# A graph layer on one core: bias of the late tiles through the early sums, key rows of two groups loaded together, loops written out

## What is computed

```python
xn = _layernorm(x)
# messages over 16 relations, summed at the destination
transformed = einsum('ni,rio->rno', xn, weight)
gnn = segment_sum(transformed[rel_type, src] * norm, dst)
# linear attention over all nodes, with a gate
q, k, v = split(xn @ Wqkv)
k = softmax(k, axis=nodes)
context = einsum('bnhd,bnhv->bhdv', k, v)
out = einsum('bnhd,bhdv->bnhv', q, context)
gate = sigmoid(gelu(xn2 @ Wg1 + bg1) @ Wg2 + bg2)
x = x + gnn + (out * gate @ Wproj + bproj)
# mixture of 8 experts, the two best of each row
x = x + moe(_layernorm(x))
```

## Time and profile before

| | us |
|---|---|
| three runs | 1664.4, 1661.96, 1661.58 |
| median of the runs | 1661.96 |
| the profiled execution, span from first to last instruction | 1663.3 |
| early tiles, per tile (from 85 to 297) | about 12.4 |
| late tiles, 22 of them from 357 to 730.7 | 373.7 |
| 22 pairs of phase two, from 843.7 to 1590.5 | 746.8 |

### The profile page before, as it was taken

One profiled execution on the slowest core, in us unless ns is written; L12 is line 12 of the kernel. 1 busy time (PEld: TensorE's weight loads), 2 busy tenths in 40 slices (PEclk: granted clock), 3 DMA queues, 4 the chain that ended last, 5 costly groups with the idle time before them and its releaser, 6 DMA issues.

```text
span 1663.3 us, 38419 instructions
## 1 busy us (share of the span) xinstructions
PE 1611.3 (97%) x10484; PEld 1452.9 (87%) x10484; DVE 1354.3 (81%) x3387; ACT 968.4 (58%) x2178; POOL 1043.2 (63%) x1134
## 2 busy tenths in 40 slices
PE   6999999999999999998699999999999999999998
PEld 5788888788888788786599999999999999999998
DVE  7978565488888888884579999999999999999985
ACT  4444222346556555553566777676767777676764
POOL 3543231577878787775677767776767766767730
PEclk9999999999999999999899999999999999999999
DMA  8676765688888888887633333333333333333320
GB/s 264 213 258 242 249 251 209 224 269 268 265 266 274 256 257 266 267 264 257 185 98 109 100 113 103 102 104 114 98 97 110 101 110 101 106 101 114 98 60 10
DMA packets 126969, 289.13 MB, mean 174 GB/s; under 512 B 21271, under 2 KB 49724, under 8 KB 126914
## 3 DMA queue, kind: packets, MB, share of 16 engines
q1 hardware_dynamic: 86068, 177.19, 29.3%
q0 software_dynamic: 39952, 110.13, 24.7%
q10 hardware_dynamic: 894, 1.16, 0.2%
HBM read 149.49 MB, written 138.90 MB: 173 GB/s over the span
## 4 chain that ended last, share of the span: by engine, by line
PE 71%; issue 8%; POOL 8%; DMA 4%; DVE 4%; ACT 2%; ACTq 0%; DVEq 0%; POOLq 0%
PE bank L1743 56%; POOL raw L673 6%; PE bank L1941 4%; DMA raw<-table,idxa 3%; PE bank L1942 3%; PE bank L1784 2%; PE bank L1785 1%; ACT mh L995 1%; POOL xres L638 1%; PE bank L1893 1%; DMA slot<-kv_d 1%; PE bank L1991 1%; PE bank L1979 1%; DVE ml L1523 1%; PE bank L1795 1%
## 5 line engine op out<-in xcount | busy, mean ns | idle before, releaser
L787 POOL DMA_INDIRECT stg<-table,idxcur x495 | 538.2, 1087 | 245.2 <-issue 111.5
L1743 PE MATMUL bank<-wreg,xt 128*128 128x512 f32 x2352 | 590.2, 402 | 4.6 <-DVE wreg L1136 1.9
L1743 PEld LDWEIGHTS bank<-wreg,xt 128*128 128x128 f32 x2352 | 436.6, 190 | 99.7 <-DVE stg L1178 2.3
L673 POOL DMA_INDIRECT raw<-table,idxa x297 | 308.6, 1039 | 86.5 <-issue 77.4
L1743 PE MATMUL bank<-tt,wreg 128*128 128x256 f32 (+1 forms) x2400 | 322.6, 284 | 2.4 <-DVE tt L1589 2.2
L1743 PE MATMUL bank<-wreg,ht 128*128 128x256 f32 x2352 | 316.8, 283 | 0.2 <-DVE ht L1639 0.2
L1743 PEld LDWEIGHTS bank<-tt,wreg 128*128 128x128 f32 x2400 | 299.8, 190 | 7.6 <-issue 7.3
L1743 PEld LDWEIGHTS bank<-wreg,ht 128*128 128x128 f32 x2352 | 295.1, 188 | 0.4 <-DVE ht L1639 0.4
L1051 ACT ACTIVATE raw<-bank,cols 128x256 f32<-128x256 f32 (+1 forms) x400 | 164.6, 462 | 105.1 <-PE bank L1743 105.1
L1523 DVE SCALAR_TENSOR_TENSOR ml<-stg,nrm,mh 128x256 fp32r<-128x256 f32 x455 | 196.1, 477 | 21.5 <-ACT mh L995 21.3
L1178 DVE COPY stg<-bank 128x512 f32<-128x512 f32 x196 | 133.4, 685 | 94.5 <-PE bank L1743 93.8
(11 more groups left out here) (236 smaller groups left out, 2151.5 us busy)
## 6 DMA issues: line engine op xcount, KB each, us to landing
table<-stg SPq DMA_DIRECT2D x196, 512.0 KB, 3.5
kv_d<-kvs SPq DMA_DIRECT2D x49, 256.5 KB, 4.5
xt_d<-xt SPq DMA_DIRECT2D x49, 256.0 KB, 4.1
xtp<-xt_d SPq DMA_DIRECT2D x24, 512.0 KB
stg<-table,idxcur POOLq DMA_INDIRECT x495
sk<-kv_d SPq DMA_DIRECT2D x24, 256.5 KB, 5.7
out_x<-xres SPq DMA_DIRECT2D x24, 256.0 KB
xres<-in_x POOLq DMA_DIRECT2D x23, 256.0 KB, 4.3
```

Of the source, the lines that this page charges most:

```text
L673: pool.indirect_dma_start(ring_a[:, r * EARLY + j, :], None, table[0:LIMIT, :], bass.IndirectOffsetOnAxis(ap=idxa[:, at:at + 1], axis=0)). ...
L787: pool.indirect_dma_start(stg[:, (s % 4) * SUP + j, :], None, table, bass.IndirectOffsetOnAxis(ap=idxcur[:, at:at + 1], axis=0)).then_inc( ...
L1743: mm = pe.matmul(dst, stat(a, c), mov(b, c), start=(n == 0), stop=(n == 3 * chunks - 1))
```

## The change

1. *Bias.* POOL's `early_gathers` no longer calls `add_bias`, so tiles 24 to 48 get no bias from POOL. DVE prepares two rows in tile 19 (`bias_rows`: high part in row 0 and low part in row 32 of `bp2`, zeros between). PE adds them by one matmul with a matrix of ones at the head of `early_sums` in odd rows, from tile BIAS_FROM = 36 on, which covers the tiles 24 to 48. `ones` becomes fp32r. DVE's `early_add` waits for POOL's bias only once.
2. *Key rows.* A new tile `later` of 14 slots lies where `wreg` begins; groups 1 and 2 are loaded into it behind group 0 without waiting for contexts. The work is cut into six parts of four or three tiles, two at slot 0 and one each at slots 1 to 4 of pair 0. The context is finished at slot 5, and the steps after it move one slot ahead. `split_hi` of the first chunk waits for all contexts. SP loads pair 0 ahead of the first two chunks. POOL's head mask and the indices of the second half of pair 0 move ahead of its gathers.
3. *Loops.* Every `Fori` of both phases becomes a Python loop, on all five engines.

```diff
+    BIAS_FROM = K2 + K2 // 2
+    BP_LO = 32
         xres = sb("xres", [P, NT, C], F32)
+        with ExitStack() as begun:
+            later = sb("later", [P, 2 * SLOTS, KVW], F32, begun)
         wreg = sb("wreg", [P, 2, 4, CC, WC, C], F32R)
...
-        ones = sb("ones", [P, P], F32)
+        ones = sb("ones", [P, P], F32R)
...
+        def group_of(part):
+            return part // 2
+        def span_of(part):
+            return (4, SLOTS) if part % 2 else (0, 4)
+        def rows_of(part):
+            g = group_of(part)
+            return slot if g == 0 else later[:, SLOTS * (g - 1):SLOTS * g]
...
-            with sp.Fori(K2 // 2 + 1, NP - 1) as i:
+            for i in range(K2 // 2 + 1, NP - 1):
...
-            def load_group(g):
-                for n, k in enumerate(group(g)):
-                    if g:
-                        sp.wait_ge(ctx_mm, HELD + SLOTS * (g - 1) + n + 1)
-                    elif n == 5:
+            def load_rows(part):
+                a, b = span_of(part)
+                for n in range(a, b):
+                    if part == 1 and n == 5:
                         sp.wait_ge(ctx1_mm, KEPT)
-                    sp.dma_start(slot[:, n, :], kv_d[k]).then_inc(kv_in[n], 16)
-            load_group(0)
+                    sp.dma_start(rows_of(part)[:, n, :], kv_d[group(group_of(part))[n]]).then_inc(kv_in[part], 16)
+            load_rows(0)
+            load_rows(1)
             first_phase_over(sp)
-            for g in range(1, GROUPS):
-                load_group(g)
-            load_chunk(4)
-            sp.wait_ge(k1_dve, 6)
-            load_chunk(5)
+            for part in range(2, 2 * GROUPS):
+                load_rows(part)
...
             load_pair(0, 2)
+            load_chunk(4)
+            sp.wait_ge(k1_dve, 6)
+            load_chunk(5)
...
-                    if r == 2:
-                        add_bias(k)
...
             first_phase_over(pool)
+            heads()
+            next_indices(0, 0, 2)
+            next_indices(0, 1, 2)
             for h in range(PIECES):
                 pool.wait_ge(tbl_st[h], 16 * NT)
...
+                if (i, s) == SPLITS[0]:
+                    act.wait_ge(ctx_mm, HELD + REST)
                 if (i, s) in SPLITS:
                     split_hi(4 + SPLITS.index((i, s)))
...
+            def bias_rows():
+                dve.wait_ge(bp_in, 16)
+                dve.memset(halves(bp2[:]), 0.0).then_inc(late_lo, 1)
+                dve.wait_ge(late_lo, 2)
+                for row in (0, BP_LO):
+                    dve.tensor_copy(bp2[row:row + 1, :], bpb[row:row + 1, :]).then_inc(late_lo, 1)
+                dve.wait_ge(late_lo, 4)
+                dve.tensor_tensor(bp2[BP_LO:BP_LO + 1, :], bpb[BP_LO:BP_LO + 1, :], halves(bp2[BP_LO:BP_LO + 1, :]),
+                                  ALU.subtract).then_inc(late_lo, 1)
...
-                dve.wait_ge(bias_in, min(t + 1, NT) if isinstance(k, int) else t + 1)
+                if isinstance(k, int) and k == K2:
+                    dve.wait_ge(bias_in, K2)
...
-            def early_sums(k, i, b, r):
+            def early_sums(k, i, b, r, biased):
...
                 pe.wait_ge(selected_a, q + 1)
+                if biased:
+                    pe.wait_ge(late_lo, 5)
+                    pe.matmul(bank[7][:, 0:C], ones[0:BP_LO + 1, :], bp2[:], start=True, stop=False)
...
-                        early_sums(k, i, b, j // 2)
+                        early_sums(k, i, b, j // 2, bias and j // 2 % 2 == 1)
...
+            for first, last, bias in ((K2 // 2 + 1, BIAS_FROM // 2, False), (BIAS_FROM // 2, NP - 1, True)):
+                for i in range(first, last):
+                    tile_pe(2 * i, i, 0, (2 * i + 1, 1), rows, bias)
+                    tile_pe(2 * i + 1, i, 1, (2 * i + 2, 0), rows, bias)
...
-                if isinstance(i, int) and (i, s) == (0, 6):
+                if isinstance(i, int) and (i, s) == (0, 5):
                     context_turn()
                     context_values()
-                if isinstance(i, int) and (i, s) == (0, 7):
+                if isinstance(i, int) and (i, s) == (0, 6):
                     query_context()
...
-GROUP_SLOTS = (0, 1, 3)
+PARTS_OF_SLOT = {0: (0, 1), 1: (2,), 2: (3,), 3: (4,), 4: (5,)}
...
-    with eng.Fori(2, pairs) as i:
+    for i in range(2, pairs):
         for s in range(8):
             slot_of(i, s, 8, i - 1, 2, i - 2, 2)
```

More of the change, by code:

```diff
@@ L575, in _ @@
             load_pair(1, 2)
-            with sp.Fori(2, NP) as p:
+            for p in range(2, NP):
                 load_pair(p, 2)
@@ L1727, in gate_bias @@
                     pe.matmul(bank[5][:, 0:G], lnbb[:, c, :], wg1_raw[:, c, :], start=(c == 0), stop=False)
-                pe.matmul(bank[5][:, 0:G], ones[0:1, :], bg1r, start=False, stop=True).then_inc(setup_pe, 1)
+                pe.matmul(bank[5][:, 0:G], halves(ones[0:1, :]), bg1r, start=False, stop=True).then_inc(setup_pe, 1)
             def query_turn():
@@ L1817, in tile_pe @@
                     pe.wait_ge(k1_dve, 1 + CC)
-                    pe.matmul(bank[7][:, 0:C], ones[:], dg1, start=True, stop=True).then_inc(k1_pe, 1)
+                    pe.matmul(bank[7][:, 0:C], halves(ones[:]), dg1, start=True, stop=True).then_inc(k1_pe, 1)
                 if isinstance(k, int) and STAGES < k <= STAGES + 3:
@@ L1874, in _ @@
             pe.wait_ge(k_shift_diag, 2)
-            pe.matmul(bank[1][:, 0:C], ones[:], dg[:], start=True, stop=True).then_inc(kmb_mm, 1)
+            pe.matmul(bank[1][:, 0:C], halves(ones[:]), dg[:], start=True, stop=True).then_inc(kmb_mm, 1)
             pe.wait_ge(add_a, ALL_ADDS)
@@ L1879, in _, with held_contexts @@
             contexts_kept(NT - 1, NP, 1, 3)
-            def contexts(g):
-                for b in range(0 if g else HELD):
+            def held_contexts():
+                for b in range(HELD):
                     pe.wait_ge(k_exp, b + 1)
@@ L1888, in contexts @@
                     mm.then_inc(ctx_mm, 1)
-                for part_no, first, last in parts(g):
-                    pe.wait_ge(k_exp, part_no + 1)
-                    for n in range(first, last):
-                        for c in range(CC):
-                            mm = pe.matmul(bank[2 + c][:, 0:XW], slot[:, n, c * P:(c + 1) * P],
-                                           slot[:, n, C:KVW], start=False, stop=(group(g)[n] == NT - HELD - 1))
-                        mm.then_inc(ctx_mm, 1)
+            def contexts(part):
+                rows = rows_of(part)
+                pe.wait_ge(k_exp, HELD + part + 1)
+                for n in range(*span_of(part)):
+                    for c in range(CC):
+                        mm = pe.matmul(bank[2 + c][:, 0:XW], rows[:, n, c * P:(c + 1) * P], rows[:, n, C:KVW],
+                                       start=False, stop=(group(group_of(part))[n] == NT - HELD - 1))
+                    mm.then_inc(ctx_mm, 1)
             def context_turn():
@@ L2037, in slot_of @@
                     if i + s == 0:
-                        contexts(0)
+                        held_contexts()
+                        for part in PARTS_OF_SLOT[0]:
+                            contexts(part)
                     if (i, s) == (1, 6):
@@ L2108, in in_slot, with run @@
                 steps[name](p, nt, *map(int, expert))
[L2111 removed]
+def run(slot_of, pairs, tail_groups):
     for s in range(8):
```

176 lines of the change are left out of this document (81 added, 95 removed).

## The result

The changed kernel takes 1634.67 us (median of 4 runs, 1631.11 to 1636.7) against 1663.18 us for the kernel before in the same set (4 runs, 1661.58 to 1665.61): a ratio of 0.9826 [0.9809, 0.9842], 28.5 us less. The profiled executions have spans of 1634.8 and 1663.3 us, so 28.5 us between them as well, and the stages of the two traces can be set side by side.

What follows compares the result with a forecast made beforehand. POOL, never resting at 16.99 us a tile, was taken to bound the late tiles. Bias 9, key rows 9 and loops 2 us summed to 20 us, off 1661.96: 1642 us, range 1630 to 1655.

Steps and rivals of the forecast that it cites:

- (a): Late tiles: taking the bias add off POOL brings a tile from 16.99 to 16.6 us, 9 us, between 4 and 14.
- (b): Hand-over: loading key rows of two groups at once completes the contexts sooner, 9 us net, between 3 and 14.
- the floor without bias: Late tiles: PE needs at least 16.13 us a tile when it adds no bias.
- The floor with bias: Late tiles from 36 on: two bias matmuls of 0.12 us each raise PE's least time to 16.37 us a tile.
- The sign that was named for (a): Late tiles: POOL waits for PE's sums, its bias group is gone, and a tile takes 16.4 to 16.7 us.
- two signs that were named for (b): Hand-over: last key-row shift before 785 less (a)'s saving; first output matmul 8 us or more nearer the late tiles' end.
- (c): All queues: written-out loops save 0.1 us a phase-two pair, 2 us in all, from 8 gained to 6 lost.
- R3: Phase two: loops were the jitter; writing them out takes 1.0 us off each pair, 22 us, giving 1622 us; chance 0.08.
- R1: Late tiles: gathers lengthen by 0.05 us in the mean, so (a) brings only 2 us, giving 1649 us; chance 0.10.
- R2: Hand-over: the burst of fourteen loads delays gathers, so (b) brings nothing, giving 1651 us; chance 0.12.
- R4: Written-out code arrives late and stops PE: 1679 us at 0.6 us a block, up to 1721 us; chance 0.05.
- R5: Late tiles stay at 17 us through another chain and contexts wait for something else, giving 1660 us; chance 0.03.

Runs made afterwards that it cites:

- second rung: The kernel before with buffers 128 bytes lower and all loops written out, bias and key rows untouched; 18.2 us less than the kernel before's 1664.34 us.

## Why the prediction was right, point by point

**The sum** was 20 us, the result 28.5. It came out on the right side and in the range, but partly by luck, by misses that cancel: parts (a) and (b) were forecast at 18 us and brought 12.2; the loops were forecast at 2 us and the placement not at all, and they brought 18.2.

**What bounds the late tiles** was right. POOL had no rest; with its add gone, PE is busy all the time and POOL waits 11.4 us for it. In the second rung, which keeps the add, POOL's groups still fill the whole stretch (370.9 of 370.3 us).

**(a), the floor without bias** was right: the prediction added up 16.13 us for a tile, and the tiles before 36 take (16.85 + 15.11)/2 = 15.98. The difference is the placement: undisturbed late tiles take 16.98 and 15.25 us in the kernels with the old one, and 16.85 and 15.11 in all with the new one, with or without (a). The allowance for jitter between two engines of nearly equal pace, which lifted this to 16.6, was not needed: once PE is the later one, most tiles repeat to 0.01 us. **The floor with bias** is the term that was mis-sized. The matmul was priced at 0.12 us from a row of 24 others of its width; it costs 0.5 us, the floor is 17.00 in place of 16.37, and the twelve tiles from 36 to 48 gain nothing. The two errors nearly cancel, 4.7 to 8.0 us for 9. The sign that was named for (a), a tile of 16.4 to 16.7 us, is met in the mean only ((160.2 + 203.6)/22 = 16.54) and by luck: no group of tiles has it, they take 15.98 and 17.00. The row that gave the price has matmuls of 128 rows, and this one has 33: the columns were compared and the rows weren't. That a smaller number of rows might cost was not weighed.

**(b)** had its mechanism right: counted from tile 48's transposes the key rows' last shift came 7.0 us sooner, and POOL's gathers, up to slot 5, then set the contexts. The step "the contexts are complete 10 to 12 us sooner" was too large. From tile 48's transposes to the values' matmuls it is 68.6, 66.6 and 68.9 us in the kernels without (b) and 60.8, 60.9 and 63.3 with it, 6.4 us in the mean. The step "I take 2 us" for the split ahead of the first output was too small: from the values to the first output it is 11.75 us in place of 8.17. In all 5.5 us at equal clock, not 9. One of the two signs that were named for (b) failed: the first output matmul was to be 8 us or more nearer to the end of the late tiles, and it is 4.1 us nearer in after (72.6 us behind tile 48's transposes in place of 76.8).

**(c)** is the step that failed. The row, 22 issue gaps and 4.7 us, was read as small and as covered by the array's queue, and only half of it was counted. It was also put at the loop's turn, where it doesn't lie: the gaps are 22.3 to 22.6 us behind a pair's gate matmuls and the branch 28.1 to 28.5, without a gap of its own. So the 0.2 us say nothing of a fetch at the branch; the trace shows none there, and no packet of instructions moves in 600 us of turns. In truth the row was one of four places in each pair, 0.43 us a pair: in a stage in which PE is busy 745.97 of 746.80 us nothing covers a pause of PE. A busy record that contains queueing doesn't show them, and this was said in the prediction of the late tiles but not applied here. R3, the loops as the jitter, priced this at 1.0 us a pair, twice its size, and its mechanism, the low parts in time, is one of the four places (0.18 us); it was given 0.08. The pair at 33.54 us in after lies under the forecast's 33.7 to 33.95 and over R3's 33.2.

**The placement** was in the diff and not in the prediction: `vea` was taken for a matter of space. It gives 3.4 us in the early tiles (323.5 to 320.1) and perhaps 1.4 more in phase two (746.9 to 745.5).

**The rivals.** R1: gathers take 1024 ns in the mean after and 1040 before, not 1.09 us; they didn't pay. R2: the distance from the late tiles to the first output shrank, by 4.1 us. R4: written out, the second rung's instruction queues moved 84 and 77 packets in place of 25 and 30, and PE shows no even gaps; no time lost to code shows anywhere. R5: the add was worth removing up to tile 36; from there on the tile stays at 17 us, as R5 said, but by the matmul that took the add's place.

## What to carry to other kernels

Price an added matmul by a row of its own form, rows as well as columns, and not by its columns alone: here 96 and 106 rows beside 128 cost nothing extra, and 33 did. Where an engine is busy for a whole stage, compare the starts of its instructions with the best spacing in the same trace: pauses of 0.1 to 0.2 us hardly appear as idle time of a busy engine (0.83 us of 746.80 here), and here they were worth more than the stall that the change was made for. And before a stage is said to be untouched, look whether its buffers move: one small buffer fewer shifted the rest by 128 bytes, and a stage with the same code changed by 1.5%.

The changed kernel may have room: at the floor of 15.98 us and with two bias matmuls of 0.12 us each, the twelve tiles from 36 to 48 would take 194.6 us in place of 203.5, 9 us less. This is an estimate, and holds only if a bias matmul of 128 rows costs what its neighbours do and POOL's own pace, (363.8 - 11.4)/22 = 16.0 us a tile, doesn't bind again; it wasn't run.

## What the runs showed of the hardware that was not expected

- A matmul of 33x256 between matmuls of 128x256: 0.20 us ahead of it and 0.31 us behind it, against 0.12 between its neighbours, whether or not it waits and whether it is first or last in the sum. One of 96x256 showed no such cost.
- The pace of matmuls depends on where buffers lie: 12.40 us for an early tile, and 12.22 with the buffers 128 bytes lower, at a full clock, on every chip seen; 989 to 991 matmuls in 212 us and 1004 to 1006.
- Kept loops cost PE 0.1 to 0.2 us at each of four places, 0.43 us in a pair of 33.9 us, and nothing at the branch itself, 608 instructions of PE a turn. Writing out all loops, with three times as many packets of instructions fetched, showed no cost.
- A microsecond at the lower clock level cost half a microsecond in the hand-over (6.9 us between two executions of the same code that differ by 13.7 us of it), and which stretches get it differs from one kernel to the next.
- The kernel before takes 1662 to 1664 us where before, after and the last set ran, and 1757 on the two chips of the first two sets. The kernel with the placement alone has pairs of 34.9 to 37.8 us there, against 33.8 to 34.2 in before. It also shows waits of ACT of up to 4.6 us in the late tiles (29.2 us ahead of its copies L837) that the profile puts down to no instruction of the kernel; the trace of before has none. The cause stays open.
